# A decoder's self attention: sums, weighted values and maxima turned by VectorE's block transposes instead of travelling through TensorE and ScalarE

## The reference, cut to what matters

```python
h   = layernorm(x)                        # [8, 512, 256]
qkv = h @ W_qkv                           # q, k, v: 16 heads of 64
p   = softmax(q @ k.T * 64 ** -0.5)       # per head 512 x 512
x   = x + concat_heads(p @ v) @ W_out     # [8, 512, 256]
```

## Time and profile before

| | |
|---|---|
| median of 3 runs | 2953.72 us (2947.42 to 3137.99) |
| the profiled execution | 2952.82 us |
| its span, first to last instruction | 2951.0 us |
| this stage, within it | 1024 to 2135 us |
| busy over the span | PE 2658.3 us (90%), PEld 1631.8 (55%), DVE 1945.2 (66%), ACT 1399.1 (47%), POOL 1107.2 (38%) |
| L1698, VectorE's reciprocals | 64 times, mean 3354 ns |
| L1660 and L1651, ScalarE's copies | 64 times 587 ns, 128 times 379 ns |
| L1574, the maxima through TensorE | 512 matmuls, mean 263 ns |

### The profile page before, as it was taken

The page is one execution under the profiler, slowest core; times in us unless marked ns, Lnnn a source line. Parts: engine busy times, 40 slices in busy tenths (PEclk is TensorE's granted clock), DMA queues, the critical chain, the costliest instruction groups (busy, mean ns, idle before and its releaser), DMA issues. The chain is left out here.

```text
span 2951.0 us, 51682 instructions
## 1 busy us (share of the span) xinstructions
PE 2658.3 (90%) x17628; PEld 1631.8 (55%) x17629; DVE 1945.2 (66%) x3269; ACT 1399.1 (47%) x2199; POOL 1107.2 (38%) x854
## 2 busy tenths in 40 slices
PE   7997899999868899999999999999889999857998
PEld 4775333333235556565656565656544454456997
DVE  4776777877668765657575656666546666574555
ACT  2433466666558653434343434343335555443333
POOL 3233323233036343435343434343443333063333
PEclk9998799999879999999999999999989999958999
DMA  5002222222111000000000000000043232146666
GB/s 163 0 0 63 61 59 61 58 61 58 30 58 44 1 1 1 1 1 1 1 1 1 1 1 1 1 1 1 1 113 81 74 79 69 37 138 230 219 211 195
DMA packets 102982, 160.60 MB, mean 54 GB/s; under 512 B 28349, under 2 KB 63432, under 8 KB 97160
## 3 DMA queue, kind: packets, MB, share of 16 engines
q1 hardware_dynamic: 97784, 147.88, 17.5%
q0 software_dynamic: 3408, 8.46, 0.8%
q10 hardware_dynamic: 1600, 1.61, 0.2%
HBM read 91.79 MB, written 14.96 MB: 36 GB/s over the span
## 5 line engine op out<-in xcount | busy, mean ns | idle before, releaser
L1678 DVE TENSOR_REDUCE self_nmax<-self_SM 128x2 fp32r<-128x1024 f32 x256 | 313.3, 1224 | 211.7 <-PE self_SM L1567 211.7
L1656 ACT ACTIVATE self_PT<-self_ST 128x1024 f32<-128x1024 f32 x256 | 262.9, 1027 | 329.4 <-PE self_ST L1592 329.4
L1723 POOL TENSOR_TENSOR self_U<-self_PT 128x1024 f32<-128x1024 f32 x64 | 153.9, 2405 | 613.5 <-ACT self_PT L1656 613.5
L499 DVE TENSOR_REDUCE cross_nmax<-cross_S 128x2 f32<-128x1024 f32 x256 | 310.7, 1222 | 110.2 <-PE cross_S L347 109.2
L444 ACT ACTIVATE cross_PT<-cross_S 128x1024 f32<-128x1024 f32 x256 | 260.0, 1023 | 123.3 <-PE cross_S L358 121.4
L1726 POOL TENSOR_TENSOR self_U<-self_U,self_PT 128x1024 f32<-128x1024 f32 x128 | 303.4, 2371 | 31.9 <-ACT self_PT L1656 27.0
L1602 PE MATMUL self_W<-self_PT,self_V 128*64 128x512 f32 x1024 | 237.4, 606 | 19.6 <-ACT self_PT L1656 14.6
L1146 DVE TENSOR_REDUCE cross_nmax<-cross_S 128x4 f32<-128x1024 f32 x128 | 156.5, 1223 | 133.4 <-PE cross_S L967 133.3
L1698 DVE RECIPROCAL self_rcp<-self_W 128x512 f32<-128x512 f32 x64 | 214.7, 3354 | 33.8 <-PE self_W L1609 33.1
L1083 ACT ACTIVATE cross_PT<-cross_S 128x1024 f32<-128x1024 f32 x128 | 131.0, 1024 | 127.6 <-PE cross_S L983 127.4
L1602 PEld LDWEIGHTS self_W<-self_PT,self_V 128*64 128x64 f32 x1024 | 72.5, 139 | 161.4 <-issue 123.2
(11 more groups left out here) (450 smaller groups left out, 7002.8 us busy)
## 6 DMA issues: line engine op xcount, KB each, us to landing
moe_staged<-in_L_ffn_W SPq DMA_DIRECT2D x36, 1024.0 KB, 6.1
cross_ks<-cross_parts SPq DMA_DIRECT2D x384, 64.0 KB, 2.3
cross_qs<-cross_parts SPq DMA_DIRECT2D x376, 64.0 KB, 2.3
all_x<-in_L_ffn_W SPq DMA_DIRECT2D x14, 1024.0 KB
all_x<-sorted_rows SPq DMA_DIRECT2D x83, 130.0 KB, 2.1
cross_cT<-in_ctx_T SPq DMA_DIRECT2D x16, 512.0 KB, 4.6
sorted_rows<-all_spare_row SPq DMA_DIRECT2D x1, 5460.0 KB, 23.8
all_x<-in_x SPq DMA_DIRECT2D x8, 512.0 KB, 4.0
```

The lines of the kernel that those rows point to most:

```text
L499: dve.tensor_reduce(nmax[:, g % 2, 0:R, n % PER_G], S[:, slot[st], :, :], AX.X, ALU.max, negate=True).then_inc(s_maxed, 1)
L1656: act.activation(PT[:, k, :, :], ST[:, :, :], ACT.Exp).then_inc(exped.sem, 1)
L1678: dve.tensor_reduce(nmax[:, i, 0:P:D], SM[:, :, :], AX.X, ALU.max, negate=True).then_inc(maxed.sem, 1)
L1723: pool.tensor_tensor(U[:, c % 2, :, :], PT[:, 0, :, :], PT[:, 1, :, :], ALU.add).then_inc(added.sem, 1)
```

## The change

- `ma` and `mb` are gone: no matmul, no ScalarE copy, no bank of `W`. VectorE's reductions write the maxima of the two heads to 8 columns of a 128x32 tile, columns 0 to 3 for head 0 and 4 to 7 for head 1. A new step **rows** follows the chunk's last reduction: VectorE turns the tile in blocks of 32x32, and SyncE issues eight transfers, each of 4 rows of 32 values, into the one partition of `mrow` that belongs to the head. `mrow` has two slots now. The first **exact** step of a chunk waits for all eight.
- `sum` and `av` are both turned by VectorE, out of PSUM, in blocks of 32x32. In a turned block the query is on the partition, so the reciprocal is needed for one column of every block: 128x16. `scale` multiplies the turned values with it and turns them back into `OT`. ScalarE's copy to `Oraw` is gone.
- TensorE's `av` waits for one exponential before each of its four parts, not for all four at its start.
- The ring `W` now carries q, k, va, vb, norm, sum, av and out.

```diff
@@ plan
                 add("exact", c * NT + k, NC * NT)
                 if k < NT - 1:
                     add("max", (c + 1) * NT + k + 1, NC * NT)
+                if k == NT - 2:
+                    add("rows", c + 1, NC)
...
-                    add("ma", c + 1, NC)
-                    add("mb", c + 1, NC)
...
-    BANKED = ("q", "k", "va", "vb", "norm", "ma", "mb", "sum", "av", "out")
+    BANKED = ("q", "k", "va", "vb", "norm", "sum", "av", "out")
@@ tensor_steps
-                elif kind == "ma":
-                    halves = [free_bank(pe, b, order, (which, n, rel)) for which in ("ma", "mb")]
-                    reach(pe, maxed, "max", b, order, ("max", n * NT + NT - 1, rel))
-                    for i in range(NT):
-                        m_up, m_low = (pe.matmul(dst[:, i * D:(i + 1) * D], nmax[rows, i, :], ident_r[rows, rows], start=True, stop=True,
-                                                 skip_group_check=True) for dst, rows in zip(halves, (UPPER, LOWER)))
...
                     if k == 0:
                         reach(pe, drained["dve"], "dve", b, order, ("k", c, rel))
-                        reach(pe, drained["act"], "act", b, order, ("mb", c, rel))
+                        rows_in(pe, b, order, c, rel)
...
                 elif kind == "av":
-                    exped.wait(pe, b, NT * (n + 1))
...
                     for k in range(NT):
+                        exped.wait(pe, b, NT * n + k + 1)
@@ scalar_steps
-                elif kind in ("ma", "mb"):
...
-                elif kind == "av":
-                    valued.wait(act, b, n + 1)
-                    scaled.wait(act, b, n - 1)
-                    act.copy(Oraw[:, n % 2, :], bank_of(order, st)).then_inc(lifted.sem, 1)
@@ vector_steps
-                    dve.tensor_reduce(nmax[:, i, 0:P:D], SM[:, :, :], AX.X, ALU.max, negate=True).then_inc(maxed.sem, 1)
+                    dve.tensor_reduce(nmax[:, i:2 * NT:NT], SM[:, :, :], AX.X, ALU.max, negate=True).then_inc(maxed.sem, 1)
+                elif kind == "rows":
+                    maxed.wait(dve, b, n_max)
+                    rowed.wait(dve, b, MROWS * n_rows)
+                    n_rows += 1
+                    dve.transpose(nmax_T[:, :].bitcast(F32), nmax[:, :].bitcast(F32)).then_inc(turned_max.sem, 1)
...
-                    dve.reciprocal(rcp[:, :], bank_of(order, st)).then_inc(done, 1)
+                    dve.transpose(turned[:, :, :].rearrange("p c x -> p (c x)"), bank_of(order, st)).then_inc(done, 1)
+                    reach(dve, drained["dve"], "dve", b, order, st)
+                    dve.reciprocal(rcp[:, :], turned[:, :, 0]).then_inc(inverted.sem, 1)
+                elif kind == "av":
+                    valued.wait(dve, b, n + 1)
+                    weighed.wait(dve, b, n - 1)
+                    dve.transpose(turned_av[:, n % 2, :, :].rearrange("p c x -> p (c x)"), bank_of(order, st)).then_inc(lifted.sem, 1)
                 elif kind == "scale":
...
-                    dve.tensor_tensor(OT[:, n, :], Oraw[:, n % 2, :], rcp[:, :], ALU.mult).then_inc(scaled.sem, 1)
+                    dve.tensor_tensor(turned[:, :, :], turned_av[:, n % 2, :, :], rcp[:, :].unsqueeze(2).to_broadcast([P, NB, BLOCK]),
+                                      ALU.mult).then_inc(weighed.sem, 1)
+                    weighed.wait(dve, b, n + 1)
+                    dve.transpose(OT[:, n, :], turned[:, :, :].rearrange("p c x -> p (c x)")).then_inc(scaled.sem, 1)
+
+        def sync_steps(sp, b, order):
+            for kind, n, rel in order.steps:
+                if kind == "rows":
+                    turned_max.wait(sp, b, order.nth["rows"][(kind, n, rel)])
+                    to = mrow[:, n % 2, :].bitcast(F32).rearrange("p (i a y) -> p i a y", i=NT, y=32)
+                    for j in range(2):
+                        for a in range(P // 32):
+                            from_ = 32 * a + NT * j
+                            sp.dma_start(to[j * D:j * D + 1, :, a, :], nmax_T[from_:from_ + NT, :].bitcast(F32)).then_inc(rowed.sem, 16)
```

More of the change, by code:

```diff
@@ L1338, in __init__ @@
         self.hT_hi, self.hT_lo = s.sb("hT_hi", [P, KC, T], F32R), s.sb("hT_lo", [P, KC, T], F32R)
[L1339 to L1340 removed]
+        self.mrow, self.ones_r, self.ones = s.sb("mrow", [P, 2, T], F32R), s.sb("ones_r", [P, P], F32R), s.sb("ones", [P, 64])
         self.half, self.eps, self.minus = (s.sb(n, [P, NT]) for n in ("half", "eps", "minus"))
@@ L1412, in plan @@
         return steps
-    BANKED = ("q", "k", "va", "vb", "norm", "ma", "mb", "sum", "av", "out")
-    FULL = ("q", "k", "va", "vb", "norm", "ma", "mb", "sum", "out")
+    BANKED = ("q", "k", "va", "vb", "norm", "sum", "av", "out")
+    FULL = ("q", "k", "va", "vb", "norm", "sum", "out")
     counted = {"ring": lambda kind: kind in FULL,
-               "act": lambda kind: kind in ("va", "ma", "mb"),
-               "dve": lambda kind: kind in FULL and kind not in ("va", "ma", "mb"),
+               "act": lambda kind: kind == "va",
+               "dve": lambda kind: kind in FULL and kind != "va",
                "split": lambda kind: kind in ("q", "k", "norm")}
-    for kind in ("exact", "max", "av", "sum", "half"):
+    for kind in ("exact", "max", "rows", "av", "sum", "half"):
         counted[kind] = lambda k, kind=kind: k == kind
@@ L1471, in self_attention @@
         guarded, maxed = loop("guarded", "max"), loop("maxed", "max")
+        MROWS = 8 * 16
+        turned_max, rowed = loop("turned_max", "rows"), Loop(s.sem("rowed"), MROWS * whole.total["rows"], MROWS * first.total["rows"])
         valued, lifted = loop("valued", "av"), loop("lifted", "av")
-        scaled = loop("scaled", "sum")
+        scaled, inverted, weighed = loop("scaled", "sum"), loop("inverted", "sum"), loop("weighed", "sum")
         added = Loop(s.sem("added"), 3 * NC)
@@ L1487, in reach, with rows_in @@
                 counter.wait(eng, b, order.prev.nth[of][st[:2] + (1,)] - counter.per)
+        def rows_in(eng, b, order, c, rel):
+            if ("rows", c, rel) in order.nth["rows"]:
+                rowed.wait(eng, b, MROWS * order.nth["rows"][("rows", c, rel)])
+            else:
+                rowed.wait(eng, b, MROWS * order.prev.nth["rows"][("rows", c, 1)] - rowed.per)
         def bank_of(order, st):
@@ L1591, in tensor_steps @@
                         at = slice(j * D, (j + 1) * D)
-                        m = pe.matmul(ST[:, j, :], ones_r[at, :], mrow[at, :], start=False, stop=True)
+                        m = pe.matmul(ST[:, j, :], ones_r[at, :], mrow[at, c % 2, :], start=False, stop=True)
                     m.then_inc(scored.sem, 1)
                 elif kind == "av":
-                    exped.wait(pe, b, NT * (n + 1))
                     dst = free_bank(pe, b, order, st)
@@ L1627, in scalar_steps @@
                 kind, n, rel = st
-                if kind in ("q", "k", "va", "norm", "ma", "mb"):
+                if kind in ("q", "k", "va", "norm"):
                     ring_full.wait(act, b, order.nth["ring"][st])
@@ L1747, in _ @@
                 scalar_steps(act, B - 1, last)
+            @block.sync
+            def _(sp):
+                sync_steps(sp, None, first)
+                for counter in (rowed,):
+                    counter.credit(sp)
+                with sp.Fori(0, B - 1) as b:
+                    sync_steps(sp, b, whole)
+                sync_steps(sp, B - 1, last)
             @block.vector
             def _(dve):
+                dve.memset(nmax[:, :].bitcast(F32), 0.0).then_inc(s_zeroed, 1)
+                dve.wait_ge(s_zeroed, 1)
                 vector_steps(dve, None, first)
-                for counter in (drained["dve"], s_stat, maxed, scaled):
+                for counter in (drained["dve"], s_stat, maxed, turned_max, lifted, inverted, weighed, scaled):
                     counter.credit(dve)
```

27 lines of the change are left out of this document (14 added, 13 removed).

## The result

The changed kernel takes 2962.72 us (median of 18 runs, 2954.3 to 2967.67) against 2953.81 us of the kernel before (median of 18 runs; one of them, at 3137.99 us, is left out of the ratio, and the others lie from 2943.06 to 2960.39). The ratio is 1.0031, 95% interval 1.002 to 1.0043. The time lies in the forecast range of 2915 to 3055 us and the sign was right, but the forecast of 2990 us was four times too large a loss: 36 us where 9 came. The profiled execution took 2954.5 us, at the fast end of its 18, with a span of 2952.7 us.

A forecast was written before the change was run, and what follows sets the result against it. PE was taken to bound the stage, with late transfers setting chunks of 15.4 us. 2952.8 + 3 (eight batches) + 3 (first chunk) + 36 (clock falls) - 4 (earlier falls) = 2991, said as 2990 us; range 2915 to 3055.

The forecast's parts named there:

- The bound and the mechanism: PE bounds the stage; the gain would be 8.2 us per batch if transfers were free, but they land after PE needs them.
- The row's time, 7.0 us: From a chunk's fourth reduction to PE: 0.1 + 0.2 + 0.03 + 7 x 0.69 + 1.83, making chunks at least 15.4 us.
- The spacing: Between SyncE's issues of a chunk's transfers: 0.69 us, taken from the cross attention's four transfers; bounds 0.61 and 1.01.
- The clock: Longer PE waits before chunks make the clock fall to half: 2.5 falls per batch of 1.8 us, 36 us over eight.
- The reason given for the price: Part of a clock fall lies in PE's wait itself, so the price was taken near the cheaper one, 1.8 us.
- Chunk 7 was to get 0.3 us shorter: Output projection hides the transfers behind chunk 7: -0.87 - 0.4 + 0.95 = -0.3 us per batch.
- my table: The sum per batch: chunks 0 to 6 change by +1.27, +0.81, 0, 0, +0.86, -1.40 and -0.84 us.
- VectorE's costs: Per chunk, three transposes of 0.705, a reciprocal of 0.254 and a small transpose of 0.2 replace 3.354 us of reciprocal.
- The 3 us ahead of the first chunk: Ahead of the stage's first chunk the row shows once, with less of V's work over it: +3 us.
- the one of quicker issues: Rival: SyncE's issues 0.61 us apart, 42 us saved, a fall in one batch of two, some 7 us: 2920; chance 0.12.
- the one in which the clock holds: Rival: the transfers are late but the clock does not fall, 2955 us; chance 0.12.
- That all would hide: Rival: transfers issue much faster, land within the 4.2 us margin, and the whole 66 us gain shows, 2887; chance 0.10.

## Why the prediction was right and wrong

1. **The bound and the mechanism: right.** PE bounds the stage; the matmuls and waits that were to leave it left (four transfers: 12.72 to 14.4 us for chunks 0 to 5, which had 14.1 to 16.8; 7.7 us per batch, 8.2 were predicted). The transfers begin after the fourth reduction and land too late, and SyncE's time to issue them is most of it: four instead of eight removes the wait, nine lengthens it by 0.6 us.
2. **The row's time, 7.0 us: the step that failed.** It measured 6.42. The spacing was 0.617 and not 0.69 us, and the landing 1.62 and not 1.83; the wait of VectorE for itself was 0.24, not 0.1. The prediction took the cross attention's spacing because the transfers were alike, several partitions into one. They are not: those are 1x8x128 values and took 0.63 us to issue, these 1x4x32 and took 0.573, and 2x4x16 took 0.495. Each 0.1 us here stands in six chunks of eight batches. The chunk was 14.77 us and not 15.4: 0.63 x 6 x 7 = 26 us for the seven batches with a next one, nearly all of the 27 us by which the forecast missed; what points 3 and 4 were wrong by nearly cancels. The run with nine transfers, where the row takes 7.0 us, shows that the chunk lengths worked out from this term were sound.
3. **The clock: right in kind, too high in number.** I had 20 falls of 1.8 us. The profile has seven behind chunk 0's wait, five behind chunk 4's and two behind the output projection's, 14 of some 1.6 us; one of 2.7 us at the stage's first exact step; and one in the last batch's chunk 6, whose price is not known. Together that is 25 us or a little more instead of 36. The profiled execution is 8 us under the median, and its mean clock, 0.953, is the highest of the 18 (0.949 to 0.953), so most executions probably had some falls more. The reason given for the price was wrong: no part of a fall lay in the wait. After chunk 0's wait the matmuls first ran at full speed for 1 us and only then at half, for 3 us. That the falls need the idle time is shown by the run that keeps PE busy. That a fall goes by the length of the wait, as the sum took it, is refuted by the run with nine: five waits of 2.64 to 2.67 us without a fall, three of 1.63 to 1.66 with one. That they would follow the wait for `OT` was not foreseen; the runs with four transfers lost up to 8 us by it until `scale` was moved.
4. **What the sum had too small, all on the slow side.** Chunk 7 was to get 0.3 us shorter and got 0.37 longer: chunk 6 needs 14.95 us on PE, more than the row, so chunk 7 keeps its wait for `nmax`, with VectorE's transpose ahead of it (0.57). The last batch, which projects nothing for a next one, has chunks of 13.9 to 14.5 us that the row stretches: its chunks 0 to 6 together took 100.2 us and now 107.5, of which 3.1 are two falls already counted, where my table had 0.7. Together these two are some 8 us and hide a third of point 2's error. The last batch is also a part of the 19 us by which the run with nine came out over the predicted time. Its profiled execution, 2997.1 us, is only 7 over; the other 12 lie between that one and the median, with a lower clock (0.943 to 0.948 in place of 0.949).
5. **VectorE's costs: right.** Transposes 0.71 (0.705 taken), reciprocal 0.253, small transpose 0.21 (0.2 taken), the output projection's wait 0.93 longer (0.95 taken). The 3 us ahead of the first chunk came as well: from the stage's second rough step to its first exact matmul it is 13.45 us (1021.86 to 1035.31), 9.47 before (1025.29 to 1034.76), 4.0 more. The fall behind it, 2.7 us, was not foreseen. In the profiled execution the stages ahead, which the change leaves alone, ended 3.4 us sooner, so the first exact matmul stands only 0.55 us later.
6. **The rivals.** Nearest in what happened came the one of quicker issues. It had the spacing right, 0.61, and four falls where 16 came: 2920. Nearest in number was the one in which the clock holds, 2955, by luck: it has the row's 7.0 us, which was too long, and no falls. That all would hide, as the figures of the Trainium skill's page DMA: Bandwidth & Descriptors (Anatomy of one DMA) lead to, is refuted by the 4.89 us of SyncE's row; its advice to coalesce small transfers (Rules for kernel authors) agrees with the run of four; the page speaks of overhead in general, and here the overhead was the time of the issues.

What stays open: why an issue's time goes with the shape, and what besides the wait decides whether the clock falls. It fell behind seven of the eight waits of chunk 0 and five of the eight of chunk 4, which are 0.1 us longer.

## What to carry to other kernels

Count the issues, not the bytes: with small transfers on one queue the data are late by the number of issues times the time of one, and that time is read from a row of the same shape. Where a fixed chain, here a reduction, a transpose and transfers, becomes longer than what TensorE has left to do beside it, every further saving on TensorE buys only idle time, and idle time of some 2 us can cost the clock besides. Split a change into its parts before judging it: of this one, the finer waits alone gave 0.7%, and together with the transfers in half as many issues 2.3%. The transposes of sums and values made each version that had them slower: 16 us with eight transfers, 12 with four, 3.5 with four and `scale` early, and 11 us (0.9975 against 0.9934) with the maxima through TensorE.

## What the hardware showed that I had not expected

- SyncE's issue time by the shape of the transfer (partitions written, rows read for each, values in a row; which side of it counts is not separated): 1x4x32 values 0.573 us, 2x4x32 and 2x4x16 both 0.495, 1x8x128 0.63; bytes did not matter between the middle two, 1 KB and 512 bytes.
- TensorE did 7 more pairs of matmuls in two chunks of each batch, and the kernel became 19 us faster.
- Waits of 1.9 to 2.1 us were followed by a clock of half in 15 of 24 places of the changed kernel, and the places repeat: chunk 1 in seven batches in a row, chunk 5 in five. With nine transfers a wait of 2.67 us passed five times at one place of the loop, while one of 1.64 us did not at another. The waits of a loop are not independent draws, so one trace's share of falls is a poor chance for another kernel's.
